# Row sums of the first attention: halvings on GpSimd and a VectorE reduction in place of TensorE products with ones

## The reference, cut to what matters

```python
score = einsum('bhqd,bhkd->bhqk', q, k) + einsum('bhqd,qkd->bhqk', q, pe_k)
attn = softmax(score, axis=-1)
ctx = einsum('bhqk,bhkd->bhqd', attn, v) + einsum('bhqk,qkd->bhqd', attn, pe_v)
ctx = ctx.transpose(0, 2, 1, 3).reshape(b, s, d)
return ctx @ W_out + b_out
```

## Time and profile before

| what | value |
|---|---|
| median of 3 runs | 2905.8 us (2904.94 to 2909.46) |
| the profiled execution | 2909.2 us |
| its span in the trace | 2907.5 us |
| PE busy, whole span | 2604.1 us, 90% |
| DVE busy | 1924.4 us, 66% |
| ACT busy | 1611.4 us, 55% |
| POOL busy | 613.6 us, 21% |
| granted TensorE clock, mean | 0.969 |

### The profile page before, as it was taken

How to read it: one execution, slowest core, us unless ns; L and a number is a source line. 1 busy time by engine, 2 the same in 40 slices (tenths; PEclk the granted TensorE clock), 3 DMA queues, 4 the chain that set the end, 5 groups by cost and what they waited for, 6 DMA issues and landing times. The chain is left out here.

```text
span 2907.5 us, 102728 instructions
## 1 busy us (share of the span) xinstructions
PE 2604.1 (90%) x42000; PEld 1971.0 (68%) x42000; DVE 1924.4 (66%) x7310; ACT 1611.4 (55%) x3731; POOL 613.6 (21%) x632
## 2 busy tenths in 40 slices
PE   4999999799988999999999999499989999998998
PEld 3777777567767777777777777377766666666666
DVE  4887788467777777777777777211117777777777
ACT  1444444366666666666666665133327666767776
POOL 2445444300110000001111111400004223322230
PEclk9999999899999999999999999699999999999999
DMA  3212100166666666666666665222321001111110
GB/s 131 103 51 73 37 15 12 36 152 148 154 151 149 152 153 148 152 155 149 152 150 153 150 149 123 86 84 98 101 72 35 24 24 29 26 24 24 28 27 9
DMA packets 341502, 268.43 MB, mean 92 GB/s; under 512 B 24602, under 2 KB 328090, under 8 KB 339516
## 3 DMA queue, kind: packets, MB, share of 16 engines
q1 hardware_dynamic: 330556, 234.82, 31.4%
q0 software_dynamic: 10496, 27.28, 3.2%
HBM read 129.88 MB, written 132.14 MB: 90 GB/s over the span
## 5 line engine op out<-in xcount | busy, mean ns | idle before, releaser
L869 DVE CUSTOM_DVE_ANT_0 neg_scores<-scores,rel_bias 128x256 f32<-128x256 f32 x1024 | 373.4, 421 | 271.7 <-PE scores L1013 226.4
L1388 ACT ACTIVATE probs<-neg_scores,low 128x256 f32<-128x256 f32 (+1 forms) x1024 | 382.5, 446 | 211.6 <-DVE low L1419 187.4
L757 ACT ACTIVATE probs<-neg_scores,low 128x256 f32<-128x256 f32 x1024 | 436.8, 500 | 42.9 <-DVE low L869 41.8
L751 ACT COPY probsT_s<-probsT 128x512 f32<-128x512 f32 x256 | 150.3, 587 | 427.6 <-PE probsT L1025 427.6
L1419 DVE CUSTOM_DVE_ANT_0 neg_scores<-scores,alibi 128x256 f32<-128x256 f32 (+1 forms) x1024 | 304.8, 354 | 109.5 <-PE scores L1466 109.2
L1025 PE MATMUL probsT<-consts,probs 128*128 128x128 f32 x2048 | 332.7, 286 | 1.3 <-ACT probsT_s L751 0.7
L1025 PEld LDWEIGHTS probsT<-consts,probs 128*128 128x128 f32 x2048 | 229.1, 143 | 72.9 <-issue 59.4
L252 POOL TENSOR_TENSOR hid<-hid,gate_bc 128x512 f32<-128x512 f32 x160 | 205.4, 1284 | 275.8 <-DVE hid L407 257.3
L876 DVE COPY rel_s<-scores 128x768 f32<-128x768 f32 x256 | 244.0, 953 | 3.0 <-PE scores L1013 1.6
L1003 PE MATMUL scores<-k_sides,q_heads 32*128 32x256 f32 x2048 | 184.3, 429 | 55.6 <-DVE rel_s L876 54.1
L1478 PE MATMUL probsT<-consts,probs 128*128 128x128 f32 x1536 | 226.8, 285 | 3.7 <-ACT probs L1388 0.4
(11 more groups left out here) (187 smaller groups left out, 5158.9 us busy)
## 6 DMA issues: line engine op xcount, KB each, us to landing
rel_rows<-rel_s SPq DMA_DIRECT2D x256, 192.0 KB
rel_bias<-rel_rows SPq DMA_DIRECT2D x256, 192.0 KB, 4.0
rel_rows<-rel_s SPq DMA_DIRECT2D x256, 128.0 KB
rel_bias<-rel_rows SPq DMA_DIRECT2D x256, 128.0 KB, 3.4
packed<-ffn_in SPq DMA_DIRECT2D x8, 1280.0 KB, 5.5
xe<-packed SPq DMA_DIRECT2D x16, 640.0 KB, 4.3
expert_out<-ye POOLq DMA_DIRECT2D x16, 640.0 KB, 6.9
xt<-xnT SPq DMA_DIRECT2D x64, 128.0 KB, 3.1
```

What stands on the lines that cost most here:

```text
L757: act.activation(probs[s % 2][:, j, :], neg[s % 2][:, j, :], ACT.Exp, bias=low[s % 3][:, j:j + 1], scale=-1.0).then_inc(exped, 1)
L869: dve.tensor_tensor_reduce(neg[s % 2][:, j, :], S_ps[:, 512 * j:512 * j + S], bias_of(s)[:, j, :], 1.0, 3e38, ALU.add, ALU.min, low[s % 3] ...
L1388: act.activation(probs[s % 3][:, j, 0:w], neg[s % 3][:, j, 0:w], ACT.Exp, bias=low[s % 3][:, j:j + 1], scale=-1.0).then_inc(exped, 1)
```

## The change

It removes the products with ones (L1045), the block of ones and its memsets. GpSimd now follows every unit: once the four exponentials are there it adds the upper 128 keys to the lower 128 (128x512 results), then the upper 64 of these to the lower 64 (128x256 results). VectorE, two steps later and behind the copy of the relative scores, sums the remaining 64 with a `tensor_reduce` into 4 sums per query. Once a batch (r = 3) VectorE takes the reciprocal of all 32 sums of a query row (128x32) and copies each to the 8 channels of its head (128x256); in `turn_a` TensorE turns these with two products against the identity into the free half of `M_ps`, and in `turn_b` VectorE multiplies the context with them. The copy of `values0` halves to 256 columns. `probs` gets a third buffer, and ScalarE waits for `halved` of the unit three steps back instead of the transposes of two back. GpSimd's indirect DMAs are issued from the same loop, behind the halvings of their step.

```diff
...
-            probs = [sm(f"probs0_{i}", [P, 4, S]) for i in range(2)]
+            probs = [sm(f"probs0_{i}", [P, 4, S]) for i in range(3)]
...
-            ctx_s = sm("ctx_s", [P, 2 * S])
-            rinv = sm("rinv0", [P, S])
+            ctx_s = sm("ctx_s", [P, S])
+            sums = [sm(f"sums0_{i}", [P, 2, 4, 4]) for i in range(2)]
+            half1 = [sm(f"half1_{i}", [P, 4, P]) for i in range(2)]
+            half2 = [sm(f"half2_{i}", [P, 4, P // 2]) for i in range(2)]
+            rinv = sm("rinv0", [P, 2, H])
+            rinv_c = sm("rinv0_c", [P, 2, H, C])
...
+                for u in range(NU0 + 5 * UB):
+                    if u < NU0:
+                        pool.wait_ge(exped, 4 * (u + 1))
+                        if u >= 2:
+                            pool.wait_ge(summed, u - 1)
+                        pool.tensor_tensor(half1[u % 2][:, :, :], probs[u % 3][:, :, 0:P], probs[u % 3][:, :, P:S], ALU.add).then_inc(halved, 1)
+                        pool.wait_ge(halved, u + 1)
+                        if u >= 2:
+                            pool.wait_ge(reduced, u - 1)
+                        pool.tensor_tensor(half2[u % 2][:, :, :], half1[u % 2][:, :, 0:P // 2], half1[u % 2][:, :, P // 2:P], ALU.add).then_inc(summed, 1)
+                    p, place = divmod(u - 5 * UB - 1, 2 * UB)
+                    if 0 <= p < nb // 2:
+                        if place == 0:
+                            rows_of(p)
+                        if place < 2 * TP:
                             pool.indirect_dma_start(
-                                out=packed, out_offset=bass.IndirectOffsetOnAxis(ap=scat[:, i, k:k + 1], axis=0),
-                                in_=xn2[p % 2][:, i, :], in_offset=None).then_inc(scattered, 16)
+                                out=packed, out_offset=bass.IndirectOffsetOnAxis(ap=scat[:, place // 2, place % 2:place % 2 + 1], axis=0),
+                                in_=xn2[p % 2][:, place // 2, :], in_offset=None).then_inc(scattered, 16)
...
                     if 0 <= s < NU0:
-                        if s >= 2:
-                            act.wait_ge(turned, 2 * (s - 2) + 2)
+                        if s >= 3:
+                            act.wait_ge(turned, 2 * (s - 3) + 2)
+                            act.wait_ge(halved, s - 2)
                         for j in range(4):
                             act.wait_ge(lowest, 4 * s + j + 1)
-                            act.activation(probs[s % 2][:, j, :], neg[s % 2][:, j, :], ACT.Exp,
+                            act.activation(probs[s % 3][:, j, :], neg[s % 2][:, j, :], ACT.Exp,
                                            bias=low[s % 3][:, j:j + 1], scale=-1.0).then_inc(exped, 1)
...
+                    u = s - 2
+                    if 0 <= u < NU0:
+                        dve.wait_ge(summed, u + 1)
+                        dve.tensor_reduce(sums[u // UB % 2][:, u % UB // 4, :, u % 4], half2[u % 2][:, :, :], AX.X, ALU.add).then_inc(reduced, 1)
...
                         if r == 1:
                             dve.wait_ge(valued, UB * b)
-                            dve.tensor_copy(ctx_s[:, :], O_ps[:, :]).then_inc(ctx_moved, 1)
+                            dve.tensor_copy(ctx_s[:, :], O_ps[:, 0:S]).then_inc(ctx_moved, 1)
                         if r == 3:
-                            dve.wait_ge(ctx_moved, b)
-                            dve.reciprocal(rinv[:, 0:P], ctx_s[:, S:S + P])
-                        if r == 6:
-                            link(dve.reciprocal(rinv[:, P:S], ctx_s[:, S + P:2 * S]))
+                            dve.wait_ge(reduced, UB * b)
+                            link(dve.reciprocal(rinv[:, :, :], sums[(b - 1) % 2][:, :, :, :].rearrange("p t j i -> p t (j i)")))
+                            if b >= 2:
+                                dve.wait_ge(spare_full, job_no["turn_b", b - 2])
+                            dve.tensor_copy(rinv_c[:, :, :, :].rearrange("p t h c -> p (t h) c"),
+                                            rinv[:, :, :].rearrange("p t h -> p (t h)").unsqueeze(2).to_broadcast((P, 2 * H, C))
+                                            ).then_inc(inverted, 1)
...
                             dve.wait_ge(spare_full, n)
-                            dve.tensor_tensor(ctx_all[:, :], M_ps[:, 0:S], ctx_s[:, 0:S], ALU.add).then_inc(spare_free, 1)
-                            dve.wait_ge(spare_free, n)
-                            dve.tensor_tensor(ctxT[:, :], ctx_all[:, :], rinv[:, :], ALU.mult).then_inc(normed, 1)
+                            dve.wait_ge(ctx_moved, b + 1)
+                            link(dve.tensor_tensor(ctx_all[:, :], M_ps[:, 0:S], ctx_s[:, :], ALU.add))
+                            dve.tensor_tensor(ctxT[:, :], ctx_all[:, :], M_ps[:, S:2 * S], ALU.mult).then_inc(spare_free, 1)
...
                     if name in ("turn_a", "turn_b"):
                         pe.wait_ge(rel_masked, 2 * b + 2)
+                        if name == "turn_a":
+                            pe.wait_ge(inverted, b + 1)
+                            for qt in range(2):
+                                pe.matmul(M_ps[:, S + qt * P:S + (qt + 1) * P], rinv_c[:, qt, :, :].rearrange("p h c -> p (h c)"), ident,
+                                          start=True, stop=True)
...
                     if name == "out":
-                        pe.wait_ge(normed, b + 1)
+                        pe.wait_ge(spare_free, job_no["turn_b", b])
...
                         for j in range(4):
                             rows = slice(32 * j, 32 * j + 32)
-                            pe.matmul(O_ps[rows, qt * P:(qt + 1) * P], v_of[b % 2][:, kt, i, rows], pt[:, j, :],
-                                      start=(u % UB == 0 and kt == 0), stop=(i == 3 and kt == KT - 1), skip_group_check=True)
-                        for j in range(4):
-                            rows = slice(32 * j, 32 * j + 32)
-                            ins = pe.matmul(O_ps[rows, S + qt * P:S + (qt + 1) * P], one_of[:, i, :], pt[:, j, :],
-                                            start=False, stop=(i == 3 and kt == KT - 1), skip_group_check=True)
+                            ins = pe.matmul(O_ps[rows, qt * P:(qt + 1) * P], v_of[b % 2][:, kt, i, rows], pt[:, j, :],
+                                            start=(u % UB == 0 and kt == 0), stop=(i == 3 and kt == KT - 1), skip_group_check=True)
                     ins.then_inc(valued, 1)
...
```

More of the change, by code:

```diff
@@ L527, in program @@
             v_of = [sm(f"v0_heads{i}", [P, KT, 4, D]) for i in range(2)]
-            one_of = sm("ones_heads0", [P, 4, 32])
             rel_s = [sm(f"rel_s{i}", [P, 4, 3 * R]) for i in range(2)]
@@ L570, in program @@
             zeros_set = semm("zeros_set")
-            ones_set = semm("ones_set")
             started = semm("counts_cleared")
@@ L588, in program @@
             ctx_moved = semm("context_moved")
-            normed = semm("context_ready")
+            halved = semm("probs_halved")
+            summed = semm("probs_quartered")
+            reduced = semm("sums_ready")
+            inverted = semm("inverse_sums_ready")
             chain = semm("dve_chain")
@@ L702, in _, with rows_of @@
                     pool.memset(v_of[i][:, :, :, :], 0.0).then_inc(zeros_set, 1)
[L703 to L708, removed]
+                def rows_of(p):
                     pool.wait_ge(slots_done, p + 1)
@@ L715, in _ @@
                     pool.wait_ge(rows_known, 2 * p + 2)
-                    for i in range(TP):
-                        for k in range(2):
-                            pool.wait_ge(lowest, 4 * min(NU0, UB * (2 * p + 5) + 2 * i + k))
+                for u in range(NU0 + 5 * UB):
[13 more added lines that the diff above has]
+                        if place < 2 * TP:
                             pool.indirect_dma_start(
-                                out=packed, out_offset=bass.IndirectOffsetOnAxis(ap=scat[:, i, k:k + 1], axis=0),
-                                in_=xn2[p % 2][:, i, :], in_offset=None).then_inc(scattered, 16)
+                                out=packed, out_offset=bass.IndirectOffsetOnAxis(ap=scat[:, place // 2, place % 2:place % 2 + 1], axis=0),
+                                in_=xn2[p % 2][:, place // 2, :], in_offset=None).then_inc(scattered, 16)
                 pool.wait_ge(scattered, 128 * (nb // 2))
@@ L899, in _ @@
                             if b < 2:
-                                dve.wait_ge(zeros_set, 3)
+                                dve.wait_ge(zeros_set, 2)
                             else:
@@ L1024, in turn @@
                     for j in range(4):
-                        ins = pe.transpose(PT_ps[:, j * P:(j + 1) * P], probs[u % 2][:, j, kt * P:(kt + 1) * P], ident)
+                        ins = pe.transpose(PT_ps[:, j * P:(j + 1) * P], probs[u % 3][:, j, kt * P:(kt + 1) * P], ident)
                     ins.then_inc(turned, 1)
@@ L1030, in value @@
                     pe.wait_ge(moved1, u + 1)
```

(2 more changed lines are left out.)

## The result

| | before | after |
|---|---|---|
| median | 2905.37 us (2902.51 to 2909.46, 4 runs) | 2931.84 us (2931.63 to 2941.17, 4 runs) |
| ratio | | 1.0100, interval 1.0084 to 1.0116 |
| profiled execution | 2909.2 us, span 2907.5 | 2931.77 us, span 2930.1 |
| granted TensorE clock, mean | 0.969 | 0.954 |

The change made the kernel 26.5 us slower, 1.0%. The forecast was 2940.5, within 2893 to 2970, and slower with 0.73.

The account below looks back on a forecast made before the run. TensorE was taken to bound plain steps, VectorE those behind the slots and Newton chains. Terms -27 + 18 + 2 + 42 = +35 on 2909.2 us gave 2944, or 2940.5 against the median; range 2893 to 2970.

Parts of the forecast that it names:

- products with ones: TensorE, between a unit's two turns: of 0.44 us removed 0.17 comes out in 160 steps, 27 us gained.
- halvings on the chains: GpSimd's halvings hold VectorE's short SBUF-to-SBUF chains: slots 17 us, Newton 15, router and normalised output 10; 42 us lost.
- two products in `turn_a`: TensorE's own path, two added products a batch: 32 x 0.55 = 18 us lost.
- reductions and other work on VectorE: VectorE: net 1.9 us a batch added, hidden except in the step with the residual add; 2 us lost.
- the ten steps in 16: First attention: steps where TensorE sets the pace, leaving out three waiting for ScalarE and three behind slots and Newton chains.
- the router and normalisation steps: VectorE's router step and normalised output: each hit by nearly 2 us, mostly covered; 0.35 us each, 29 times, 10 us lost.
- The lock misses the chains: Rival: halvings run beside VectorE's chains without holding them; -7 us, 2899, or 2888; chance 0.17.
- The reduction is held too: Rival: VectorE's reduction behind L876 stands 1.3 us in most steps; 77 us more, 3017; chance 0.04.
- Half a loss: Rival: the three stretches lose 10 to 18 us and the gain covers them; 2903 to 2910; chance 0.08.
- The clock falls more often: Rival: more waiting brings one or two more TensorE clock falls in 16 steps; 16 to 32 us more, 2956 to 2973; chance 0.12.
- a slow spell in every batch: Sign that the forecast is wrong: a slow spell of TensorE's clock in every batch.

Follow-up runs that it names:

- run 1: Kernel before with the products with ones of batches 1 to 31 left out, nothing added, later row sums stale: 2859.66 us, ratio 0.9862.
- run 6: Kernel before without the products with ones (but for the first batch) and with GpSimd's halvings on an unread scratch tile: 2912.32 us, ratio 1.0035.
- run 2: Kernel before plus GpSimd's two halvings of every unit, on a scratch tile nobody reads: 2925.34 us, ratio 1.0087.
- run 3: Changed kernel with one more wait, so that halvings run beside VectorE's row minima: 2883.63 us, ratio 0.9941 to the kernel before.
- run 5: Kernel before plus two unread products of identity with identity ahead of `turn_a`, nothing removed: 2911.20 us, ratio 1.0039.
- run 7: Changed kernel with late halvings, VectorE's reductions left out from the third batch on, later sums stale: 2873.95 us, ratio 0.9908 to the kernel before.
- Run 8: Changed kernel with late halvings, TensorE taking the relative values before the second turn instead of behind it: 2859.73 us, ratio 0.9851 to the kernel before.

## Why the prediction was right

The direction and the place were as forecast, and so was the main cause, the halvings beside VectorE's chains. The sum, +35 us, was 8.5 too high, and that it came so near is in part luck: its terms were off in both directions, and a rival that it left out, the clock, came true beside them.

| term | predicted | measured |
|---|---|---|
| products with ones | -27 | -40.8 (run 1) |
| halvings on the chains | +42 | +52.7 with the ones gone (6 less 1); +24.9 with them (2); +43 moved away (3 against the change) |
| two products in `turn_a` | +18 | +10.6 (run 5) |
| reductions and other work on VectorE | +2 | +9.7, the reductions alone (3 less 7) |
| sum | +35 | +32.2 by the runs, +26.5 in fact |

**Products with ones.** The step that put 0.17 us on the gain of a unit was mis-sized. I took the wait between copy and turn as 0.14 us, from the turn that follows the second copy, and the later of two starts of the first copy; it is 0.05 [the plain step above], and 1.54 to 1.28 makes 0.26. With 155 units of the ten steps in 16 that is 40 us, run 1's figure. The ten steps are not shown by themselves: in run 1's trace nine of the sixteen places in the pattern are shorter, by 0.2 to 0.7 us. That the wait for the copy caps it was right: runs 1 and 8.

**Halvings.** Slots lost 1.1 us against my 1.2, Newton's two instructions 0.9 against 1.0, and the first step behind (L816, 1.3 us more) went as sketched. Over the whole, 42 us lies between what the halvings cost with the ones in place, 24.9 with hardly a change of the clock, and the 52.7 with the ones gone, of which an estimated 7 to 14 are the clock's. The sum had one price for both; that it depends on the length of TensorE's step is what runs 2 and 6 show. Which steps made the difference is open: the 10 us that I left for the router and normalisation steps were not measured apart.

**Two products.** Priced at full length, 18; 10.6 measured. The two steps themselves grew by 0.99 us in 16 against my 1.10; the rest of the difference may be the clock's (run 5).

**VectorE's own work.** 0.41 us a reduction was exact (410 ns). That it costs nothing outside one step is not borne out: 9.7 us in run 7, but with 2 to 17 as what the two runs allow. The reciprocal took 343 ns where I took 0.35, the copy behind it 293 in the median, where I took 0.41; both are off the path.

**The rivals.** "The lock misses the chains" fell with the durations above, and with run 2. "The reduction is held too" fell with run 3: 252 of 256 started inside a halving, and none took over 421 ns. "Half a loss" was priced wrongly: -7 with a loss of 10 to 18 gives 2909 to 2917 and not 2903 to 2910, and the lock would have had to cost under 7 us, not under 14, for the kernel to be faster.

"The clock falls more often" came true, and with it one of my own signs of being wrong, a slow spell in every batch: there are two in every two batches. The windows of one cycle of 16 steps, two batches, show it (kernel after; the third number from the end is the clock):

```profile
1483.00:1496.00 13.00, 11.48 (x167) 8.07 (x164) 10.98 (x48) 7.89 (x18) 7.18 (x10) 0.78 0.59 142
1496.00:1505.00 9.00, 6.65 (x145) 4.97 (x146) 7.87 (x26) 5.41 (x12) 5.32 (x6) 1.00 0.54 136
1505.00:1512.00 7.00, 7.00 (x169) 5.41 (x166) 4.53 (x15) 2.65 (x6) 2.98 (x4) 0.76 0.64 152
```

There are two spells partly at the lower of the two levels, one behind each stretch in which TensorE stood for VectorE; in the kernel before there was at most one in such a cycle, behind the slots. Summed over the stage TensorE was at the lower level for 46 us before, 142 in the changed kernel, and 60 with late halvings (run 3), each in its profiled execution. What that costs can be estimated from cycles of the same trace, which run the same work. First two of the changed kernel, then two of run 2:

```profile
1535.71:1615.68 79.97, 68.70 (x1468) 51.24 (x1467) 64.65 (x245) 48.44 (x110) 40.31 (x43) 0.96 0.61 148
1615.68:1696.18 80.50, 69.83 (x1468) 52.06 (x1467) 64.85 (x245) 48.44 (x110) 40.30 (x43) 0.94 0.61 149
```

```profile
1611.41:1690.19 78.78, 70.24 (x1719) 54.96 (x1720) 62.25 (x229) 48.56 (x110) 40.29 (x42) 1.00 0.62 151
1054.93:1134.78 79.85, 72.22 (x1719) 56.15 (x1720) 62.29 (x227) 48.80 (x110) 40.30 (x42) 0.98 0.61 149
```

Over the thirteen whole cycles of each trace behind step 39, one more microsecond at the lower level goes with 0.15 to 0.3 us more time in most traces. By that estimate the clock has 14 to 29 of what the changed kernel lost against the one before, and 12 to 24 of run 3's 43 us; my 16 to 32 was a fair price, at a chance of 0.12. That it only follows the waits for VectorE is argued. Run 8 speaks against it as a full account: with late halvings and the shortest time of all it has 101 us at the lower level. No run held the clock and changed the waits, so the division stays an estimate. That the lock costs time without the clock is shown, by run 2.

The remainder, 32.2 by the single runs against 26.5, is within what four differences can miss, and open beyond that. The terms were measured on different backgrounds, and run 6 shows that they don't add; its 52.7 holds clock time as well.

## What to carry to other kernels

Before work goes to an idle GpSimd, look at what VectorE does at that very moment: beside instructions that read PSUM it is free (563 of the 1024 row minima of the changed kernel start inside a halving, and none takes over 427 ns), beside short chains from SBUF to SBUF it holds a link until it is done itself, and one wait can move it from the second to the first (43 us here). And price a removal by the next wait behind it: of 0.44 us taken from TensorE 0.26 came out until the order of its work was changed.

## What the runs showed of the hardware that I had not expected

- A copy of ScalarE and the TensorE turn that waits for it were 0.05 us apart (1497.40 to 1497.45), a third of what I had read from another pair of instructions.
- What GpSimd does decides what it holds: beside memsets of 524 and 311 ns in the median the Newton instruction with two SBUF inputs stayed at 165 ns at most, while a cast from SBUF to SBUF rose to 466 ns in the median; beside tensor-tensor halvings both were held, to 619 and 1239 ns at most.
- The `tensor_reduce` stayed within 409 to 421 ns where 252 of 256 started inside a halving (run 3), and within 402 to 417 where only 55 had one beside them (kernel after).
- More work on TensorE went with less time at the lower level of its clock: with the two products added (run 5) there was none in the stage behind the first 20 us, against 27 before. Halvings beside shorter TensorE steps went with more: 94 us in the whole stage in run 6, 46 in run 1.
